# Projections and attention of a transformer layer in one block: the last pair's keys first, the first pair's keys and queries read back between its remaining products

## The reference, cut to what matters

```python
h = layernorm(x)                                     # [2048, 512]
q_lat, kv_lat = h @ Wq_down, h @ Wkv_down            # widths 256 and 128
q = concat(q_lat @ Wq_up, rope(q_lat @ Wq_rope))     # per head 64 + 64
k = concat(kv_lat @ Wk_up, rope(h @ Wk_rope))
v = kv_lat @ Wv_up
x = x + concat_heads(softmax(mask(q k^T / sqrt(128))) v) @ Wo
n = layernorm(x)
x = x + (silu(n @ q3(W_up).T) * (n @ q3(W_gate).T)) @ q3(W_down).T
```

## Time and profile before

| what | value |
|---|---|
| median of 3 runs (lowest, highest) | 1926.53 us (1924.0, 1930.52) |
| the profiled execution | 1928.58 us |
| its span, first to last instruction | 1926.8 us |
| mean granted TensorE clock | 0.983 of 2.4 GHz |
| latents | 0 to 74 us of the span |
| heads_inputs | 74 to 289 us |
| turnover, until attention runs steadily | 289 to 340 us |
| attention | 340 to 1539 us |
| feed_forward | 1539 to 1926.8 us |

### The profile page before, as it was taken

How to read it: one execution, slowest core, us unless ns; L and a number is a source line. 1 busy time by engine, 2 the same in 40 slices (tenths; PEclk the granted TensorE clock), 3 DMA queues, 4 the chain that set the end, 5 groups by cost and what they waited for, 6 DMA issues and landing times. The chain is left out here.

```text
span 1926.8 us, 31082 instructions
## 1 busy us (share of the span) xinstructions
PE 1847.7 (96%) x10898; PEld 1608.6 (83%) x10898; DVE 1335.8 (69%) x2818; ACT 1037.7 (54%) x2486; POOL 524.5 (27%) x315
## 2 busy tenths in 40 slices
PE   6899994999999999999999999999999889999998
PEld 4788872898998999999999999999999778787777
DVE  5466663788888888888888888888888643333333
ACT  2232333677777767666676667667666432323232
POOL 4456661111121145235234234334233000000000
PEclk9999995999999999999999999999999999999999
DMA  3399994521321222221212212112111060000000
GB/s 118 119 235 225 220 226 108 161 86 49 92 77 61 66 61 71 68 64 53 72 41 65 72 50 66 54 57 78 34 50 40 17 257 1 22 0 22 2 20 22
DMA packets 97821, 154.18 MB, mean 80 GB/s; under 512 B 12704, under 2 KB 46624, under 8 KB 97696
## 3 DMA queue, kind: packets, MB, share of 16 engines
q1 hardware_dynamic: 86176, 131.58, 23.3%
q10 hardware_dynamic: 11520, 20.98, 4.3%
HBM read 97.98 MB, written 54.53 MB: 79 GB/s over the span
## 5 line engine op out<-in xcount | busy, mean ns | idle before, releaser
L1016 ACT CAST turned_hi<-ps_turn 128x512 fp32r<-128x512 f32 (+1 forms) x576 | 313.1, 570 | 276.7 <-PE ps_turn L1202 273.5
L1008 ACT ACTIVATE probs<-ps_scores,bias 128x512 f32<-128x512 f32 (+3 forms) x640 | 401.1, 639 | 62.9 <-DVE bias L1102 62.6
L1107 DVE TENSOR_TENSOR turned_lo<-ps_turn,turned_hi 128x512 fp32r<-128x512 f32 (+1 forms) x576 | 374.8, 656 | 67.3 <-ACT turned_hi L1016 61.7
L1202 PE MATMUL ps_turn<-ident,probs 128*128 128x128 f32 x2176 | 301.8, 273 | 4.9 <-DVE turned_lo L1107 4.9
L1099 DVE TENSOR_REDUCE negmax<-ps_scores 128x1 f32<-128x512 f32 x384 | 262.1, 686 | 53.8 <-PE ps_scores L1186 49.9
L1202 PEld LDWEIGHTS ps_turn<-ident,probs 128*128 128x128 f32 x2176 | 256.3, 140 | 37.7 <-issue 6.4
L942 POOL TENSOR_TENSOR q_lo<-q_raw,q_hi 128x512 fp32r<-128x512 f32 x64 | 82.8, 1293 | 719.2 <-ACT q_hi L1037 719.2
L1186 PE MATMUL ps_scores<-k_hi,q_hi 128*128 128x512 f32 (+2 forms) x576 | 235.6, 409 | 27.1 <-POOLq L950 18.3
L1221 PE MATMUL ps_o<-turned_hi,kv_hi 128*128 128x256 f32 x1088 | 227.0, 285 | 2.0 <-DVE o_lo L1113 2.0
L1221 PE MATMUL ps_o<-turned_lo,kv_hi 128*128 128x256 f32 x1088 | 223.9, 282 | 0.0
L1221 PE MATMUL ps_o<-turned_hi,kv_lo 128*128 128x256 f32 x1088 | 223.8, 282 | 0.0
(11 more groups left out here) (146 smaller groups left out, 3503.6 us busy)
## 6 DMA issues: line engine op xcount, KB each, us to landing
plainT<-plain_out ACTq DMA_DIRECT2D x64, 256.0 KB, 4.1
rotT<-rot_out SPq DMA_DIRECT2D x64, 256.0 KB, 4.3
all_signs<-signs SPq DMA_DIRECT2D x24, 512.0 KB, 2.8
q_raw<-plainT SPq DMA_DIRECT2D x128, 64.0 KB, 2.4
q_raw<-rotT SPq DMA_DIRECT2D x256, 32.0 KB, 2.1
signs<-in_W_up SPq DMA_DIRECT2D x16, 512.0 KB, 3.6
signs<-in_W_gate SPq DMA_DIRECT2D x16, 512.0 KB, 3.6
signs<-in_W_down SPq DMA_DIRECT2D x16, 512.0 KB, 3.6
```

What stands on the lines that cost most here:

```text
L1008: nc.scalar.activation(probs_of(n, i)[:, h, first_key:first_key + keys], ps_scores[:, pieces.number[args] % RING, 0:keys], ACT.Exp, scale= ...
L1016: nc.scalar.copy(turned[0][:, at, cols(*args)], ps_turn[:, bank, cols(*args)]).then_inc(turned_hi_ready, 1)
L1107: nc.vector.tensor_tensor(turned[1][:, at, cols(*args)], ps_turn[:, bank, cols(*args)], turned[0][:, at, cols(*args)].bitcast(F32), ALU.su ...
L1202: last = nc.tensor.transpose(ps_turn[:, bank, (2 * b + h) * P:(2 * b + h + 1) * P], probs_of(n, i)[:, h, key:key + P], ident[:])
```

## The change

`heads_inputs` and `attention` no longer open blocks of their own. Each returns one function per engine, and `program` runs the two one after the other in one block, so no engine waits for the others between them. Their SBUF and PSUM are laid over one another by hand (`places`): the split keys of pair 0 lie where `xT_hi` is, the split queries, `probs0` and the mask where `xT_lo` is, `turned` where `kvT` is; `q_raw` and the new `first_raw` (16 KB a partition, all 2048 raw keys of pair 0's two heads) where the raw pair weights and the even pairs' split weights are. The projections' PSUM is that of attention: `ps_turn` for rotated products, `ps_o` for plain ones, the last bank of the scores' ring for `wvo`.

The loop over the pairs has three turns; pairs 6 and 7 stand behind it. Pairs 0 to 6 keep their order of work (`usual_order`). Pair 7 has its own (`last_order`), which every engine walks, each doing its own kinds:

```diff
+def last_order():
+    order = []
+    for c in range(NC):
+        order += [(VO_HI, c // 2)] * (c % 2 == 0)
+        order += [(ROT, c, 0)]
+        order += [(EARLY, 0)] * (c == 0)
+        order += [(VO_LO, c // 2)] * (c % 2 == 0)
+        order += [(VO, c // 2)] * (c % 2 == 1)
+    order += [(EARLY, 1), (ROT, 0, 1), (EARLY, 2), (PLAIN, 0, 0), (PLAIN, 0, 1), (EARLY, 3)]
+    order += [(ROT, 1, 1), (EARLY, 4), (PLAIN, 1, 0), (PLAIN, 1, 1)]
+    order += [(ROT, 2, 1), (PLAIN, 2, 0), (PLAIN, 2, 1), (EARLY, 5)]
+    return order + [(ROT, 3, 1), (PLAIN, 3, 0), (PLAIN, 3, 1)]
```

```diff
+    def early_sync(sp, stage):
+        if stage == 0:
+            load_qk(sp, 1, 0, slice(0, T), first_raw[:], first_loaded)
+            load_slot(sp, 0, 0)
+        if stage == 1:
+            load_slot(sp, 1, 0)
+            sp.dma_start(mask[:], hbm["mask"]).then_inc(mask_loaded, 16)
+            load_w(sp, 0, 0)
+            sp.sem_inc(w_raw_free, 1)
+    def early_gpsimd(pool, stage):
+        if stage in (1, 3):
+            n = stage // 2
+            split_lo(pool, 0, "split_q", (n,), n + 1)
+    def early_scalar(act, stage):
+        def first(c):
+            act.wait_ge(first_loaded, 48)
+            for h in range(2):
+                raw, hi, _ = first_views(c, h)
+                nc.scalar.copy(hi, raw).then_inc(first_hi_ready, 1)
+        if stage == 1:
+            split_hi(act, 0, "split_q", (0,), 0)
+            first(0)
+            first(1)
+        if stage == 3:
+            first(2)
+            first(3)
+            split_hi(act, 0, "split_q", (1,), 0)
+        if stage == 5:
+            for f, kind, args in plan.of(-1):
+                if first_head(kind, args) and kind == "exp":
+                    soften(act, args, f - 1)
+    def early_vector(dve, stage):
+        if stage in (2, 4):
+            for c in (stage - 2, stage - 1):
+                for h in range(2):
+                    raw, hi, lo = first_views(c, h)
+                    dve.wait_ge(first_hi_ready, 2 * c + h + 1)
+                    nc.vector.tensor_tensor(lo, raw, hi.bitcast(F32), ALU.subtract).then_inc(first_ready, 1)
+        if stage == 5:
+            dve.wait_ge(mask_loaded, 16)
+            for f, kind, args in plan.of(-1):
+                if first_head(kind, args) and kind == "maximum":
+                    maximum(dve, args, f - 1)
+    def early_tensor(pe, stage):
+        if stage == 5:
+            for f, kind, args in plan.of(-1):
+                if first_head(kind, args) and kind == "scores":
+                    scores(pe, args, 0, f, 1)
```

`first_head` picks the four pieces of tile 15 for head 0. `body(-1)` leaves these out and is otherwise as before; its first turn now waits until the projections' PSUM banks are free. The splits of pair 0's `wvo` move from `FIRST_SPLITS` into the list of pair 0, since their room is still the projections', and SP's loads of `y` change places:

```diff
+        self.only[0] += [(2.0 + 3 * h, 0, "split_w", (h,)) for h in range(2)]
...
+        sp.wait_ge(keep["stores_issued"], 1)
...
         for s in (*keep["rot_stored"], *keep["plain_stored"], keep["wvo_stored"]):
             sp.wait_ge(s, 16)
...
+        load_y(3)
+        load_y(0)
+        body(-1, skipped=(("load_q", 0), ("load_q", 1), ("load_w", 0), *(("load_k", c) for c in range(NC))))
+        load_y(2)
+        load_y(1)
```

More of the change, by code:

```diff
@@ L726, in upto, with attention @@
         return self.n * following + self.number[args] + 1 + self.late
-def attention(nc, hbm, keep):
+def attention(ctx, nc, hbm, keep, at, banks):
     y, kv, ident, abs_sums, scale, bound = (keep[n] for n in ("y", "kv", "ident", "abs_sums", "scale", "bound"))
@@ new lines, in attention @@
+    mask = at("mask", [P, PIECE])
+    signs = at("signs", [P, WCH])
+    below = at("below", [P, WCH], BF16)
+    ps_scores, ps_turn, ps_o = banks
+    ps_out = ps_o[:, 1, :]
+    sign_loaded = sem("sign_loaded")
+    compared = sem("compared")
+    abs_loaded, abs_done = sem("abs_loaded"), sem("abs_done")
+    abs_summed, scale_done, bounds_ready = sem("abs_summed"), sem("scale_done"), sem("bounds_ready")
+    signs_ready = sem("signs_ready")
+    signs_stored = sem("signs_stored")
+    y_loaded = [sem(f"y_loaded{m}") for m in range(NC)]
@@ new lines, in maximum @@
+    def maximum(dve, args, following):
+        n, i, h, p = args
+        t = SLOTS[n][i]
+        keys = piece(t, p)[1]
+        scores = ps_scores[:, pieces.number[args] % RING, 0:keys]
+        one = npieces(t) == 1
+        to = bias[:, n % 2, 2 * i + h:2 * i + h + 1] if one else negmax[:, h, p:p + 1]
+        told = bias_ready if one else max_done
+        dve.wait_ge(scores_ready, pieces.upto(args, following))
+        if last_piece(*args):
+            nc.vector.tensor_tensor_reduce(scores, scores, mask[:, PIECE - keys:], -1.0, -NEG,
+                                           ALU.add, ALU.min, to).then_inc(told, 1)
+        else:
+            nc.vector.tensor_reduce(to, scores, AX_X, ALU.max, negate=True).then_inc(told, 1)
+        if last_piece(*args) and not one:
+            dve.wait_ge(max_done, partial.upto(args, following))
+            nc.vector.tensor_reduce(bias[:, n % 2, 2 * i + h:2 * i + h + 1], negmax[:, h, 0:p + 1],
+                                    AX_X, ALU.min).then_inc(bias_ready, 1)
@@ new lines, in scores @@
+    def scores(pe, args, j, f, back):
+        n, i, h, p = args
+        t = SLOTS[n][i]
+        keys = piece(t, p)[1]
+        if (i, h, p) == (0, 0, 0):
+            if n == 0 and not back:
+                pe.wait_ge(k_ready, k_splits.upto((NC - 1, 1), f))
+            pe.wait_ge(q_ready, q_splits.upto((n,), f - back))
+        if back:
+            pe.wait_ge(first_ready, 2 * p + h + 1)
+        pe.wait_ge(exp_done, softened.upto(args, f - back))
+        wide = max(keys, 2 * P)
+        for m, (x, z) in enumerate(parts(0, 1)):
+            last = nc.tensor.matmul(ps_scores[:, pieces.number[args] % RING, 0:wide],
+                                    q[n % 2][x][:, 2 * i + h, :],
+                                    k_of(j, z, h, p)[:, 0:wide],
+                                    start=(m == 0), stop=(m == 2))
+        last.then_inc(scores_ready, 1)
```

1354 lines of the change are left out of this document (692 added, 662 removed).

## The result

The median is 1920.03 us over 4 runs (1918.14 to 1922.49), against 1926.53: a ratio of 0.9963, with an interval of 0.9948 to 0.9978. The change gains 6.5 us. The forecast was 15.2, and 1920.03 lies above its range. The profiled execution took 1922.49 (span 1920.7), so it is 6.1 faster than the profiled execution of before (span 1926.8).

The account below looks back on a forecast made before the run. TensorE, busy 96% of the span, was taken as the bound, so only its waits, as between projections and attention, could be won: 22.3 - 5.0 - 2.1 = 15.2 us, from 1926.53 to 1911.3, range 1903 to 1918.

Parts of the forecast that it names:

- First wait, 3.3: Pair 7, before the first head's `VO` product: PE waits 3.3 us for the split of its factors.
- Second wait, 7.7 at half clock: Pair 7, before the second head's `VO`: PE waits 7.7 us for factors queued behind early loads, then runs at half clock.
- my 2.95 MB: Bytes on SP's queue up to and including pair 7's second head's factors, taken at 241 GB/s, so landing at 280.0.
- my upper bound for the landing, 281.7: Latest landing of pair 7's second head's factors, with 0.26 MB of ACT's added, at 229 GB/s.
- 22.3 gained at `values`: Start of steady attention: its first product, `values`, comes at 315.8 instead of 338.09, 22.3 us gained.
- ACT's wait for slot 2, 6.0, PE's 5.0: Early attention: ACT waits 6.0 us for the queries of slot 2, and PE loses 5.0 waiting for a scores bank.
- Half clock 2.1: Early attention, after PE's idle 5 us: the clock falls to half, 2.1 us lost, bounds nothing and twice that.
- What costs nothing: Turnover into attention: late key stores, plain copy 4, POOL's queries split and loads of `y` 3 and 0 cost nothing.
- my signs of being wrong on a wait: Wrong if the wait at the second `VO` is under 4 or over 12 us, or ACT does not wait for slot 2.
- The queue and the clock cost more: Rival, chance 0.17: factors land at 281.7, PE loses 6.0, half clock lasts twice as long; gain 9.8 us, 1916.7.

Follow-up runs that it names:

- e1: Changed kernel with the load of `signs` issued right behind the loads of `y` 3 and 0: 1910.36 us, ratio 0.9913.
- e2: Changed kernel with the queries of slot 2 loaded before the loads of `y` and `load_w` of head 1: 1917.12 us, ratio 0.9946.
- e8: Kernel before the change, with only its load of `signs` issued ahead of the four loads of `y`: 1925.62 us, ratio 0.999.
- e4: Changed kernel with the edits of e1, e2 and e3 together: 1900.64 us, ratio 0.9868.
- e6: Changed kernel with the edits of e1 and e2, and pair 7 reordered so both `wvo` products come after more key or plain products: 1901.6 us, ratio 0.9863.
- e9: Kernel of e6 with one more rotated and one more plain product of pair 7 ahead of the casts of the first keys: 1904.67 us, ratio 0.9881.
- e10: Kernel of e4 run once more, unchanged: 1904.81 us, ratio 0.9878.
- e11: Kernel of e6 run once more, unchanged: 1902.72 us, ratio 0.9876.
- e3: Changed kernel with pair 7's second head's `wvo` factors loaded ahead of the nine early loads of keys and queries: 1916.25 us, ratio 0.994.
- e7: Kernel of e5 with the edits of e1 and e2: 1918.17 us, ratio 0.9947.
- e5: Changed kernel with pair 7 in the usual order and all six early stages behind its last product, blocks still joined: 1932.22 us, ratio 1.0018.

## Why the prediction was wrong

Step by step, in the words of the prediction:

- **First wait, 3.3**: measured 2.9. Right.
- **Second wait, 7.7 at half clock**: measured 8.1, and the clock 0.50 from 284 to 290. Right, but two errors cancel in it, which is luck: the cast starts at 283.34 where I had the factors landing at 280.0 (280.8 on this trace's clock, which is 0.84 later), while PE came to its wait later too, since it had run at half clock from 270 to 273, after the first wait of 2.9, where I had full clock. In e1 and e2, which kept full clock there, the same wait is 9.5. From the end of the store's issue at 268.3 to 283.3 my 2.95 MB are 197 GB/s, under the 241 that I took from the earlier trace rows and past my upper bound for the landing, 281.7 (282.5 on this clock). The Trainium skill ("DMA: Bandwidth & Descriptors", Bandwidth) gives 341 GB/s for a transfer of 1 MB to 128 partitions; by it the factors would have landed at 276.4. The key loads, most of these bytes, fill 64 and 32 partitions, so its condition is not met, and the trace shows no such rate. The trace agrees with its rule of ring order (same page, Queues, rings and completion order): 3.5 us of landing became 9.4 behind the keys.
- **22.3 gained at `values`**: measured 19.2 from the zero. Against pair 7's first product (260.30 before, 261.14 after) PE comes to the second `VO` 2.0 later than forecast (24.6 for 22.6) and to the scores of tile 0 4.1 later (51.9 for 47.8). I had the second head's scores follow the projections without a gap; they waited 1.9 for a bank that ACT's exponentials had to free (the row at 307.82), and ACT itself had waited 4.2 for DVE's maxima (306.90), which stand on DVE behind the subtractions of the keys and a rotated product. I had made ACT the chain here, and it was DVE. (The next wait, 2.2 before the scores of tile 0, was in the forecast with 1.9.) From there to `values` it was 1.0 faster than forecast, which leaves 3.1.
- **ACT's wait for slot 2, 6.0, PE's 5.0**: measured 5.1 and 3.4. Right in place and kind, a little large. **Half clock 2.1**: with `signs` out of the way in both kernels, PE's stretch from `values` to the first `add` is 24.0 for 19.4, so both terms together cost 4.6 where I had 7.1. I had the gain at `values` 3.1 too large and these losses 2.5 too large, which nearly cancels: that 15.2 is close to what e8 and e1 show without the wait for `signs` is in part luck.
- **"What costs nothing"** is the step that failed. I asked of the loads of `y` 3 and 0 whether they would be in before `load_w`; I did not ask what stands behind `y` 2 and 1, and put it at nothing. Before, all four went out in one issue of 2.5 us at 333.4, and behind them, as after, the queries of slot 3, a chunk of keys and `signs` (the prediction names the loads of `y` alone); after, `y` 2 and 1 are sent at 329.00 and the rest follows. All of it still stands on SP behind `load_w` of head 1 (issued at 325.12), which waits for POOL's split of head 0, the very link that I had priced for the queries of slot 2. The load of `signs` took 9.3 us to land (10.1 before). It was issued 7.6 earlier than before (343.04 to 335.42), but ACT, which had gained more, came to it 14.1 earlier (350.45 to 336.34, the start of the cast less the idle time). The difference, less 0.8 in the landing, is the growth of the wait from 2.70 to 8.36. The sum should have had this wait as a term. I had the earlier trace rows in hand, with 10.1 for this very load, and used it to argue about another one. None of my signs of being wrong on a wait came up, since none of them looked at this one.

With its numbers: 15.2 forecast; e8 and e1 put the change without the wait for `signs` at 13.9 from the zero; the growth of that wait takes 5.5 of it, which leaves 8.4; the feed-forward stage takes 1.5, which leaves 6.9; the later zero takes 0.85, and so the two profiled executions differ by 6.1 (the medians by 6.5). Of the rivals, none had this mechanism. "The queue and the clock cost more" is nearest in kind, a load behind others on SP's queue, but in another place.

That the feed-forward stage is 1.5 longer in the profile (388.3 to 389.7 from the last `add`) does not go with the change. In the thirteen profiles here it has one of two lengths: 388.0 to 388.3 in six (before, e4, e6, e9, e10, e11) and 389.7 to 390.1 in seven, among them e8, which is the old kernel with one load moved. In the six the granted clock of the first 15 us behind the last `add` is 0.62 to 0.67, in the seven it is 0.50. What decides between the two was not tried.

What stays open: how far the last pair's order can still be bettered. e3, e6 and e9 each removed or shortened a wait of PE there, and each time 2 to 8 us of another came in its place. A split of the first keys that takes less of ACT and DVE, a load of them in chunks, or a second buffer for `wvo`'s store was not tried.

## What to carry to other kernels

When a change brings an engine to a place earlier, list all loads that this engine will meet behind it, those of background work too, and ask for each when it is issued, behind what on its queue, and who stands behind the engine that waits. An in-order engine makes the most unhurried load urgent. Interleaving (15 to 17 us from e7 to e4) and early issue (14.0 from e5 to e7) were both needed here: joining the blocks gave nothing by itself (1.0018), and 0.5% once the two late loads were out of the way (0.9947).

## What the runs showed of the hardware

- **One execution's profile has an offset that is not the kernel's.** The zero stood between 256.9 and 262.8 in kernels that do the same work up to there; the unchanged kernel of e4 had it at 256.91 and 260.81. All of it arises in the first 91 us: from pair 0's first `wvo` product (at 85.5 to 91.3) to the zero it is 171.42 or 171.43 us in all thirteen profiles. In e4 the clock was 1.00 from 30 to 40 us, in e10 0.83, and the projections start 1.6 later; the other 2.3 are a wait of PE before its third rotated product, 0.48 in e4 and 2.80 in e10. Such an offset is as large as half the effect sought: spans of single profiles can mislead by 4 us. A zero behind the common part takes most of it out; what is left between two profiles of one kernel is 0.7 (e4, e10) and 1.7 (e6, e11). By spans, e4 gained 22.0 on after; by the zero, 16.9 to the last `add`.
- **The same wait of 2.9 us cost the clock in one execution and not in another.** After the first wait before `wvo` PE worked without a gap in both after and e1. In after the granted clock from 270 to 273 was 0.50; in e1 it was 1.00 from 268 to 272. Here it made no difference to what follows: the second `wvo` product starts 25.3 after the zero in after and 25.2 in e1, since the wait before it takes up the rest. The waits of 8.1 and 5.7 in after were each followed by half clock (rows 284 to 290 and 346 to 352). The Trainium skill ("TensorE: Matmul & The Clock Gate", HAM oscillation) describes a kernel whose clock drops with each wait for a transfer between bursts of matmuls; with the two long waits the trace agrees. The waits on that page are longer than the short one here, which went either way.
- **The same load lands in 3 or in 9 us by its place on the queue.** The 320 KB of `vo_raw` took 3.5 in the median of before and 9.4 behind the keys; ahead of them it took 3.0 and 3.1 (e3, e4). Stores that ACT issues among such loads are late as well: the 256 KB of `wvo` took 4.1 in the median of before's projections and 12.7 in e3.
